# Routing the first group's tokens early, and three smaller moves of work, in a multi-layer transformer kernel on one core

## The reference, cut to what matters

```
for l in 0..3:
    x = x + tanh(g_xattn[l]) * xattn_l(layernorm(x), ctx)
    x = x + tanh(g_ffn[l])   * ffn_l(layernorm(x))
```

## Time and profile before

| what | value |
|---|---|
| runs shown | 1667.19, 1672.74, 1675.39 us; median 1672.74 |
| the profiled execution: its own time | 1668.5 us |
| its span in the profile | 1667.1 us |
| PE busy | 1542.2 us, 93% of the span |
| DVE, ACT, POOL busy | 755.4, 670.7, 242.0 us |
| DMA moved | 156.38 MB, mean 94 GB/s |

### The profile page before, as it was taken

One profiled execution on the slowest core, in us unless ns is written; L12 is line 12 of the kernel. 1 busy time (PEld: TensorE's weight loads), 2 busy tenths in 40 slices (PEclk: granted clock), 3 DMA queues, 4 the chain that ended last, 5 costly groups with the idle time before them and its releaser, 6 DMA issues.

```text
span 1667.1 us, 32135 instructions
## 1 busy us (share of the span) xinstructions
PE 1542.2 (93%) x12101; PEld 1272.1 (76%) x12101; DVE 755.4 (45%) x2649; ACT 670.7 (40%) x2136; POOL 242.0 (15%) x378
## 2 busy tenths in 40 slices
PE   7999999799989999998699978999999999999986
PEld 5787887688977777775588876778988777777764
DVE  3535565411026676864011157770124443444476
ACT  2615433222107676654233325643334443344432
POOL 2022210000001121212311133155000000000000
PEclk9999999799999999998799999989999999999999
DMA  9600011359310100401799810337930001000000
GB/s 309 227 1 1 1 42 38 114 188 302 53 53 2 55 2 2 181 2 35 240 309 317 298 35 24 103 102 245 300 101 1 1 1 38 1 1 2 1 1 23
DMA packets 103253, 156.38 MB, mean 94 GB/s; under 512 B 12231, under 2 KB 80959, under 8 KB 102535
## 3 DMA queue, kind: packets, MB, share of 16 engines
q1 hardware_dynamic: 97515, 143.53, 26.4%
q0 software_dynamic: 3552, 9.18, 1.6%
q10 hardware_dynamic: 2048, 1.84, 0.3%
HBM read 147.31 MB, written 11.67 MB: 95 GB/s over the span
## 4 chain that ended last, share of the span: by engine, by line
PE 70%; ACT 7%; DVE 6%; DMA 5%; issue 3%; POOL 2%; POOLq 0%; ACTq 0%; DVEq 0%
PE psum L579 43%; PE psum L676 6%; PE psum L660 6%; PE psum L700 5%; PE psum L966 4%; ACT arena L887 4%; DMA arena<-token_rows 3%; DMA expert_out<-arena 1%; PE psum L535 1%; POOL token_rows L1269 1%; PE psum L953 1%; ACT arena L901 1%; PE psum L708 1%; DVE arena L799 1%; PE psum L1669 1%
## 5 line engine op out<-in xcount | busy, mean ns | idle before, releaser
L887 ACT ACTIVATE arena<-arena,rowmin 112x375 f32<-112x375 f32 (+1 forms) x584 | 292.5, 507 | 184.9 <-DVE rowmin L799 184.7
L579 PE MATMUL psum<-arena,region 128*128 128x112 f32 (+2 forms) x1920 | 325.7, 326 | 5.8 <-DMA arena<-in_ctxT 2.4
L579 PEld LDWEIGHTS psum<-arena,region 128*128 128x128 f32 x1920 | 261.3, 196 | 67.7 <-issue 6.7
L579 PE MATMUL psum<-region,arena 128*125 128x128 f32 (+4 forms) x1632 | 231.6, 292 | 9.6 <-DVE arena L788 3.5
L579 PEld LDWEIGHTS psum<-region,arena 128*125 128x125 f32 (+2 forms) x1632 | 196.5, 184 | 43.8 <-issue 18.7
L676 PEld LDWEIGHTS psum<-identity,arena 112*125 112x125 f32 (+1 forms) x1240 | 142.1, 177 | 59.6 <-ACT arena L901 17.2
L676 PE MATMUL psum<-identity,arena 112*125 112x112 f32 (+1 forms) x1240 | 165.1, 278 | 18.0 <-DVE arena L811 8.0
L579 PE MATMUL psum<-arena 128*128 128x128 f32 (+4 forms) x896 | 141.4, 315 | 0.0
L660 PE MATMUL psum<-arena 32*112 32x375 f32 (+3 forms) x912 | 133.9, 479 | 0.5 <-DVE arena L777 0.4
L579 PEld LDWEIGHTS psum<-arena 128*128 128x128 f32 (+2 forms) x896 | 125.7, 191 | 10.6 <-issue 0.3
L947 POOL COPY arena<-rinv 112x128 f32<-112x128 f32 x136 | 34.1, 295 | 582.3 <-DVE rinv L822 559.5
(11 more groups left out here) (302 smaller groups left out, 1889.8 us busy)
## 6 DMA issues: line engine op xcount, KB each, us to landing
stream<-in_moe_w SPq DMA_DIRECT2D x36, 1024.0 KB, 7.3
arena<-in_moe_w SPq DMA_DIRECT2D x36, 1024.0 KB, 7.4
arena<-in_ctxT SPq DMA_DIRECT2D x32, 375.0 KB, 4.3
stream<-in_e_wg SPq DMA_DIRECT2D x8, 512.0 KB, 4.6
stream<-in_e_wu SPq DMA_DIRECT2D x8, 512.0 KB, 5.7
stream<-in_e_wd SPq DMA_DIRECT2D x8, 512.0 KB, 6.6
region<-in_e_wg SPq DMA_DIRECT2D x8, 512.0 KB, 7.7
region<-in_e_wu SPq DMA_DIRECT2D x8, 512.0 KB, 8.7
```

Source lines behind the costliest of these rows:

```text
L579: last = pe.matmul(dst, l, r, start=(i == 0), stop=(i == n - 1))
L887: last = act.activation(e, e, ACT.Exp, bias=rowmin[:, j, n:n + 1], scale=-1.0, accum_out=rowsum[:, j, h:h + 1])
```

## The change

1. **Scatter by group.** Every expert now owns a fixed region of 7 chunks (`MAX_OF`) in `tok_rows`, plus one spare chunk for all. The slots of the first group need no counts of the second any more. They are computed after the second group's attention (`slots_of(0)`: one counting product, one ACT copy, three products of half the width on PE, three DVE instructions between `norm_stats` and `norm_apply`). POOL scatters the first 8 pairs, then waits for `slots_of(1)` and scatters the others.
2. **Chunks by table.** Since chunks are no more packed, their address comes from a table `tok_base` in SBUF. POOL reads it with a `value_load` before each row load and before each store. SP loads the second chunk's expert before it waits for the scatters.
3. **Zero fills.** `tok_rows` and `tok_outs` have 57 chunks each. The first fill is where both were; the second comes behind the contexts of xattn_1's second group.
4. **Contexts.** Lanes 1 to 3 of xattn_2's first contexts are loaded before the wait for the shared expert (two arena tiles change places for it). Lane 0 stays where it was.
5. **Causal copies by step.** In steps in which DVE has other work (`between`), ACT takes the first bank's copy: f0 group 0 steps 1, 2, 4, 5; f1 group 0 steps 4, 5, 6; both second groups step 1.
6. **Rounding.** ACT rounds all four rows of the first group and rows 1 and 3 of the second. The second group's transposes and products use two PSUM banks each, in another order.

The core of the diff:

```diff
-            g.wait_ge(s_route, 8)
-            g.wait_ge(*p["normed"].at(0, f_norms(0)[NORM_B2], LANES - 1))
-            for b in range(B):
-                for k in range(TOP2):
+            for i in range(ITERS):
+                g.wait_ge(s_route, 5 if i == 0 else 9)
+                g.wait_ge(*p["normed"].at(0, f_norms(0)[NORM_A2 + i], LANES - 1))
+                for j in range(LANES):
+                    for k in range(TOP2):
...
             def chunk_rows(it, r):
-                g.dma_start(tok_x[r % 2], tok_rows[bass.ds((it * TOK_SLOTS + r) * P, P), :]).then_inc(s_xr[r % 2], 16)
+                at_ = g.value_load(tok_base[0:1, bass.ds(it * TOK_SLOTS + r, 1)], min_val=0, max_val=SPARE * P)
+                g.dma_start(tok_x[r % 2], tok_rows[bass.ds(at_, P), :]).then_inc(s_xr[r % 2], 16)
...
                         wait_first(g, *p["tok_y_kept"].at(it, n))
-                        g.dma_start(tok_outs[bass.ds((it * TOK_SLOTS + n) * P, P), :], tok_y[n])\
+                        at_ = g.value_load(tok_base[0:1, bass.ds(it * TOK_SLOTS + n, 1)], min_val=0, max_val=SPARE * P)
+                        g.dma_start(tok_outs[bass.ds(at_, P), :], tok_y[n])\
...
+            def slots_of(i, to):
+                of = slice(i * P // 2, (i + 1) * P // 2)
+                held_by = slice(0, (i + 1) * P // 2)
+                pe.matmul(to[0:T, 0:P // 2], before, picked[:, of], start=True, stop=False)
+                pe.matmul(to[0:T, 0:P // 2], count[held_by, :], groups_before[held_by, of], start=False, stop=False)
+                pe.matmul(to[0:T, 0:P // 2], whole_of.broadcast_to([E2, T]), chunks_before[:, of], start=False,
+                          stop=True).then_inc(s_rmm, 1)
...
                     project_out(pe, p, it, 0, w_f[l][3], lambda j: p["o_T"].at(it, af[l].tiles - 1), onto=True)
+                    if l == 0 and it:
+                        pe.wait_ge(s_picks, TOP2)
+                        pe.matmul(bank[4][0:P // 2, 0:T], picked[:, 0:P // 2], one_col[0:T, 0:1].broadcast_to([T, T]),
+                                  start=True, stop=True).then_inc(s_rmm, 1)
+                        pe.wait_ge(s_rconst, 16 * 7)
+                        pe.wait_ge(s_route, 2)
+                        slots_of(0, bank[5])
...
                 norm_stats(v, p, 0, n, summed_out, lambda j: p["proj_out"].at(it, 0, j))
+                if l == 0 and it:
+                    slots_of(0, bank[5], 2, 2)
                 norm_apply(v, p, 0, n, summed_out, dst)
...
             chunk_expert(0, 0)
+            chunk_expert(0, 1)
             sp.wait_ge(s_scat, 16 * PAIRS)
-            for r in range(1, TOK_SLOTS):
+            for r in range(2, TOK_SLOTS):
...
+            for j in range(1, LANES):
+                context("l2", 0, j)
...
-                    if r % a.steps + 1 < a.steps:
+                    if r % a.steps + 1 < a.steps and (between is None or r not in between):
...
-                    attend_scalar(act, af[l], p, it)
+                    attend_scalar(act, af[l], p, it, own=(1,) if it else ((1, 2, 4, 5), (4, 5, 6))[l])
...
+            def round_rows(it, j):
+                act.wait_ge(*p["tiny_done"].at(0, H_TINY_AT[it] + 4))
+                act.activation(h_rows[it][j], h_rows[it][j], ACT.Identity, bias=round_col[0:T, :],
+                               scale=tinies[it][:, 12, j:j + 1]).then_inc(p["rounded"].sem, 1)
...
-            round_hidden(1, 0)
-            for j in range(1, LANES):
-                round_hidden(1, j)
-                quantize_hidden(1, j - 1)
-            quantize_hidden(1, LANES - 1)
-            for j in lanes_of:
-                keep_hidden(1, j)
-                if j:
-                    add_ffn(1, j - 1)
-            add_ffn(1, LANES - 1)
+            v.wait_ge(*p_l3f["tiny_done"].at(0, H_TINY_AT[1] + 4))
+            quantize_hidden(1, 0)
+            quantize_hidden(1, 1)
+            keep_hidden(1, 0)
+            quantize_hidden(1, 2)
+            keep_hidden(1, 1)
+            quantize_hidden(1, 3)
+            add_ffn(1, 0)
+            keep_hidden(1, 2)
+            add_ffn(1, 1)
+            keep_hidden(1, 3)
+            add_ffn(1, 2)
+            add_ffn(1, 3)
```

More of the change, by code:

```diff
@@ L891, in keep_probs @@
             def keep_probs(r):
-                if a.whole_pairs and r % a.steps + 1 < a.steps:
+                if a.whole_pairs and r % a.steps + 1 < a.steps and r not in own:
                     return
@@ L1072, in _ @@
             load(tok_rows.rearrange("(c p) f -> c p f", p=P),
[L1073 to L1076, removed]
+                 A["zeros"].unsqueeze(0).broadcast_to([SPARE + 1, P, C]), s_zero)
             def expert(e, s):
@@ L1093, in _ @@
                 context("l1", 1, j, p_l1x["v_out"].at(0, a1.tiles - 1, j))
+            load(tok_outs.rearrange("(c p) f -> c p f", p=P), A["zeros"].unsqueeze(0).broadcast_to([SPARE + 1, P, C]),
+                 s_zero)
             sp.wait_ge(*end["l1x"])
@@ L1121, in _ @@
                 for j in range(LANES):
-                    context("l2", it, j, p_l2x["v_out"].at(0, a2.tiles - 1, j) if it else None)
+                    if it or j == 0:
+                        context("l2", it, j, p_l2x["v_out"].at(0, a2.tiles - 1, j) if it else None)
                     if it:
@@ L1235, in rstds_twice @@
             def rstds_twice(group):
-                of, n = slice(group * LANES, (group + 1) * LANES), 3 + 5 * group
+                of, n = slice(group * LANES, (group + 1) * LANES), 4 + 5 * group
                 a, b = tiny[:, 15, :], tiny[:, 18, :]
@@ L1523, in _ @@
                     square_of(u - 1)
+                    for j in range(LANES):
+                        round_rows(0, j)
                 relu_of(u)
@@ L1527, in _ @@
             square_of(2 * UNITS - 1)
+            for j in (1, 3):
+                round_rows(1, j)
         @block.tensor
@@ L1954, in turn_hidden @@
                 for c in range(8):
-                    last = pe.transpose(turn_bank[:, c * T:(c + 1) * T], hq[j][:, c * P:(c + 1) * P],
+                    last = pe.transpose(turn_banks[it][j % 2][:, c * T:(c + 1) * T], hq[j][:, c * P:(c + 1) * P],
                                         ident_bf[0:T, 0:T])
@@ L1959, in down_of @@
             def down_of(it, j):
-                pe.wait_ge(*p["x_added"].at(it, 0, j - 1))
+                if it == 0 or j != 1:
+                    pe.wait_ge(*p["x_added"].at(it, 0, j - 1 - (it if j else 0)))
                 pe.wait_ge(*p["q2T_ready"].at(it, 0, j))
-                matmuls(pe, down_bank[0:T, 0:C], [(hqT[j][:, c, :], w_td[:, c, :]) for c in range(8)])\
+                matmuls(pe, down_banks[it][j % 2][0:T, 0:C], [(hqT[j][:, c, :], w_td[:, c, :]) for c in range(8)])\
                     .then_inc(p["proj_out"].sem, 1)
@@ L1993, in _ @@
             keep_busy(pe, bank[5], 20)
-            for j in range(LANES):
+            turn_hidden(1, 0)
+            for j in range(1, LANES):
                 turn_hidden(1, j)
-                if j:
-                    down_of(1, j - 1)
+                down_of(1, j - 1)
             down_of(1, LANES - 1)
@@ L2294, in summed_out, with slots_of @@
                 return bank_s[j][0:T, 0:C]
+            def slots_of(i, src, products, done):
+                of, half = slice(i * SEQ_ITEMS, (i + 1) * SEQ_ITEMS), P // 2
+                v.wait_ge(s_rmm, products)
+                v.tensor_tensor(place[:, of, :], src[0:T, 0:half].rearrange("t (g e) -> t g e", e=E2), picks[:, of, :],
+                                ALU.mult).then_inc(s_route, 1)
+                v.wait_ge(s_route, done + 1)
+                v.tensor_reduce(placef[:, of], place[:, of, :], AX_X, ALU.add).then_inc(s_route, 1)
+                v.wait_ge(s_route, done + 2)
+                v.tensor_copy(tok_slot[:, of], placef[:, of]).then_inc(s_route, 1)
             def second_norm(p, l, it, dst):
@@ L2507, in keep_hidden @@
                     v.wait_ge(*p_l3f["proj_out"].at(0, 0, j))
[L2508 removed]
+                v.tensor_scalar(hqT[j], three(turn_banks[it][j % 2][:, 0:8 * T], 8), -128.0, None, ALU.max)\
                     .then_inc(p_l3f["q2T_ready"].sem, 1)
```

113 lines of the change are left out of this document (63 added, 50 removed).

## The result

The changed kernel takes 1718.61 us (median of 4 runs, 1715.32 to 1720.89), the kernel before 1669.97 (4 runs): ratio 1.0282, 95% interval 1.0255 to 1.0309. The forecast was 1657. The profiled execution has a span of 1718.0 us, 50.9 more than before.

The account below looks back on a forecast made before the run. PE's chain, 70% of the span, bounds the kernel; stretches where PE isn't the chain count. Terms sum to -13.6: 1668.5 gives 1654.9, plus 2 for the median, 1657; forecast 1652 to 1661, whole range 1648 to 1668.

Parts of the forecast that it names:

- Zero fills: The two fills on SP's queue: cost nothing, being covered; without that cover the second would cost 25 us.
- Reads of the address table: POOL's reads in the chunk loop: +1.8 us (0 to 7.2), and +0.4 before the last store.
- Rival 1: The chunk loop's reads show in full: +7.2 for +1.8, so 1662 us; chance 0.18.
- Rival 4: Slower: a read on POOL costs much more than on SP, a loss from 0.86 us a read; chance 0.10.
- The quarter: Share of the chunk loop's 7.2 us of reads taken to show, the rest hidden under weights in flight: +1.8.
- Scatter by group: Scatters and start of the chunk loop: first pair of chunks 11.7 us earlier, bounds -9 and -13.
- the clock's 1.9: First pair of chunks: 1.9 of the 11.7 us gained come from PE at full clock.
- Rival 2: The scatters don't overlap, POOL's first eight go no earlier: -11.7 shrinks to -1, so 1668 us; chance 0.07.
- rival 3: Loop start: first row loads stand behind the experts, 7 to 8 us given back, 1664 us; chance 0.12.
- Causal copies: Copies on ACT: f0's first group +1.4 us (0 to 1.6), f1 -1.6, second groups gain 0.1 each at most.
- contexts: Context loads of xattn_2, lanes 1 to 3 ahead: -0.2 us (0 to -1), lane 0's wait not moved.
- Rounding: Last block: -3.2 us in the second group, one transpose 0.5 earlier in the first, together -3.7 (-2 to -5).

Follow-up runs that it names:

- after_60: The changed kernel with 60 chunks in place of 57 in both tensors and fills, the fills at its places: ratio 0.999 to the kernel before, 1668.41 us.
- before_reads: The kernel before with POOL reading one unused number of the expert table ahead of each row load and store of the chunk loop: ratio 1.0070.
- best_behind: best with the second expert of the first turn issued behind the wait for the scatters: ratio 0.9926 to the kernel before.
- best: fills_late with the reads of reads_hidden and DVE, not ACT, doing the causal copies in f0's first group: ratio 0.9918 to the kernel before, again 0.9931.
- fill_rows: The changed kernel with both zero fills written by partition, outermost count 128 in place of 57: ratio 1.0034 to the kernel before.
- reads_hidden: fills_apart with POOL's row table reads put ahead of waits that outlast them, one read a turn still in the open: ratio 1.0029 to the kernel before.
- best_60: after_60 with the reads of reads_hidden and without ACT's four copies in f0's first group: ratio 0.9908 to the kernel before, 1651.76 us.
- fills_late: The changed kernel with its 57-chunk fills moved, first behind layer 0's second contexts, second behind xattn_2's second masks: ratio 0.999 to the kernel before.
- fills_apart: fill_rows with the first fill moved behind the second contexts of layer 0: ratio 1.0071 to the kernel before.

## Why the prediction was wrong, point by point

**Zero fills: the step that failed.** The text had "10 us at 300 GB/s" for the first and "25 us from 268" for the second, "cost nothing". Measured: some 90 us each at 82 GB/s, +22.0 and +28.3. I looked for cover in the slices' DMA share, and took the rate from slices in which SBUF was loaded. No row showed a fill of 57 chunks; those that did run there had 26 and 8. The cover was misread too: the contexts of layer 0's second group are first used at 123.52 before, not at 94, and went out only at 134.36. The bound of 25 us that I named for lost cover was for one fill and at the wrong rate, and the range left it out. What the runs put in its place: the outermost count, 57, gives 3 engines (share 0.19, 3 packets in flight), 60 gives 15 (15 in flight, 356 GB/s with the other traffic of the stretch), and after_60 shows that this alone is the 50 us.

The Trainium skill (DMA: Bandwidth & Descriptors, section "Why a DMA increments its semaphore by 16 and not by 1") states the rule: a transfer runs on the largest number of engines up to 16 that divides the slowest dimension of both sides. By that rule 57 = 3 x 19 gives 3, 60 gives 15 and 26 gives 13; the packet records agree with all three (13 in flight in the kernel before from 45 to 51, while its 26 chunks are filled, then 8 for its 8). It was on a page that I cited for something else.

**Reads of the address table: mis-sized.** Predicted +1.8 and +0.4 (bounds 0 and 7.2); measured +11.6 over the loop, outside the bounds. Rival 1 was right that they show in full. Rival 4 was right that a read costs more on POOL than the 0.45 taken from SP, but not in its size, 0.86 us and up: a read is 0.29 us of load and up to two of 0.15 of arithmetic and with its issue 0.61 us on POOL (0.68 to 1.29). 16 of them are 9.8 us; the other 1.8 of the 11.6 are open. The quarter rested on two pairs of offsets and the thought that a row load lands when SP's weights do. before_reads refutes it: row loads issued later landed later, median 5.9 us from issue in both.

The Trainium skill (DMA: Bandwidth & Descriptors, "Queues, rings and completion order") had said so: an engine takes turns between queues with work. The runs agree: that median of 5.9 us didn't shrink.

**Scatter by group: right in kind, -6.7 for -11.7.** First scatter 116.6 us behind the end of xattn_2 before and 106.4 after, 1.26 apart without a gap: 9.8 earlier was predicted, 10.2 came. The rest was lost behind the last scatter. It lands in 5.54 us, not 2.56, beside two experts' weights; with one of them behind (best_behind against best) 1.6 of these 3.0 us come back, and for the rest no run gives the cause. The first row load needs two reads where it needed one (2.19 us from the landing, not 1.44). And the clock's 1.9 didn't come: the first pair takes 9.15 us, PE's granted clock is 0.63 in 860 to 865, behind a wait of 4.28 us. I had counted on a full clock. Rival 2 didn't happen, the 16 scatters go at 1.26 us each with DVE at work. Nor did rival 3: SP issues the third expert 1.5 us ahead of the first row load, and that takes 6.13 us, 6.36 before.

**Causal copies, contexts.** f0's first group +0.7 for +1.4, its second -0.4 for nothing; f1 -1.3 for -1.6. (The text took 0.54 us for DVE's copy too; its row says 0.61.) Contexts 0 for -0.2: PE still waits 2.5 us for lane 0 in after_60.

**Rounding: -2.8 for -3.7, the size right by luck.** In the second group the first rounding starts at 1706.40, on ACT, and the last addition is 8.5 us away, 13.5 before:

```profile
1706.40 2.38 ACT L1539 ACTIVATE arena<-arena,round_column 112x1024 f32<-112x1024 f32 x2 [2.97 <-DVE arena L2552]
```

```profile
1714.86 0.48 DVE L2576 SCALAR_TENSOR_TENSOR x_state<-psum,arena,x_state 112x256 f32<-112x256 f32 x1 [0.44 <-PE psum L586]
```

That is -5.0 for the -3.2 that I took. I had counted on half clock; granted is 1.00 in 1706.4 to 1715, where 1655 to 1660 had 0.51 before. But the second group gets there 2.0 us later. PE's clock does that, and the same code runs without it. 20 dummy products between the groups, first in the changed kernel's profile, then in that of the same kernel run again (after_again):

```profile
1685.75 4.32 PE L542 MATMUL psum<-identity 128*128 128x128 f32 x20
...
1686.69 2.40 PE L542 MATMUL psum<-identity 128*128 128x128 f32 x20
```

Granted are 0.52 and 1.00 in 1685 to 1690. With the eight products ahead of them that is 2.8 us. Where the clock stays up the second group starts 0.7 us earlier than before, as the text had it for the first group (0.5), and the last block is 5.5 us shorter: so in after_again, after_60, fill_rows, reads_hidden and best_60. In the other profiles with this last block the dip is there and the block 2.7 to 3.0 us shorter; nothing here shows what decides it. The edit is worth 5.5, outside the bounds of 2 to 5, less whatever the clock takes back.

With the fills right the forecast would still have been 11 us too low: after_60 takes 1668, no change. What the sum had right in kind was paid back by the reads.

## What to carry to other kernels

Factor the outermost count of every transfer you add or resize, and price a fill by the engines that this leaves it, not by bytes over the rate of the stretch; then ask what stands behind it in the queue, for a queue holds back later loads long before they are needed. An index read per step cost in full here, on a queue that works in order: put it ahead of a wait that outlasts it, not on the other side of the same store. And name the price of lost cover in the range, not only in the text.

## What the runs showed of the hardware that I had not expected

- A fill with one row of 1 KB to a packet moved 110 and 119 GB/s at shares of 0.74 and 0.52, and PE stopped for 10.1, 10.2, 11.5, 8.0, 7.0 and 6.2 us in six profiles beside such fills, with no wait in the profile. A fill of 5% more bytes in 120 packets of 64 KB, at 356 GB/s, stopped nobody. The Trainium skill (Runtime: NRT & Kernel Launch, section "Instruction fetch mechanics") says that sequencers fetch their code by a DMA queue of their own, a block at a time. The traces agree: each stop ends 1.2 to 1.5 us behind the landing of a 16 KB packet of an instruction queue; the packet that is next in order behind 58 us starts at 74.3 in fills_late and at 91.4 in fills_apart.
- One slow transfer shows up as a 75 us issue of a load that stands a few places behind it. The name on that row, an expert's weights, is not the cause.
- The same code met PE's lower clock in some executions and not in others: 20 dummy products took 4.32 us at a granted clock of 0.52 in one profile and 2.40 at 1.00 in the next. A stage's gain read from one profile can be off by that much.
